# Biases folded into the projection weights, and evacuation of query/key and attention banks in one instruction each

## The reference

```
n   = layernorm(x)                           # no gain, no offset
Q,K,V = n W_Q^T + b_Q, n W_K^T + b_K, n W_V^T + b_V     # 16 heads of 64
A   = softmax(Q K^T / 8) V                   # per head, 256 x 256 scores
x1  = x + layernorm(sum over heads of A W_O + b_O)
m   = layernorm(x1)
gate = softmax(m G^T);  t = m U^T            # 8 experts, rank 16
z   = m W^T + (1/16) sum_e gate_e t_e V_e
out = x1 + layernorm(z)
```

## Time and profile before

| | |
|---|---|
| median of 3 runs | 1256.75 us (1256.18 to 1256.93) |
| the profiled execution | 1255.58 us, its span 1253.8 us |
| busy share of the span | TensorE 96%, VectorE 90%, ScalarE 83%, GpSimd 57% |
| mean granted TensorE clock | 0.990 |
| chain of work that ended last | TensorE 63%, VectorE 25%, issue 7%, GpSimd 3%, ScalarE 1% |

### The profile page before, as it was taken

One profiled execution on the slowest core, in us unless ns is written; L12 is line 12 of the kernel. 1 busy time (PEld: TensorE's weight loads), 2 busy tenths in 40 slices (PEclk: granted clock), 3 DMA queues, 4 the chain that ended last, 5 costly groups with the idle time before them and its releaser, 6 DMA issues.

```text
span 1253.8 us, 33748 instructions
## 1 busy us (share of the span) xinstructions
PE 1200.7 (96%) x10496; PEld 967.9 (77%) x10496; DVE 1124.9 (90%) x3305; ACT 1039.4 (83%) x3465; POOL 712.7 (57%) x805
## 2 busy tenths in 40 slices
PE   5999999999999999999999999999999999999994
PEld 4777787777787787887778787778887777887773
DVE  6799999999999999999999999999999999999993
ACT  6888888888888888889888888888889888889881
POOL 2456655666655666655666555666555566556552
PEclk9999999999999999999999999999999999999997
DMA  6000000000000000000000000000000000000000
GB/s 209 1 2 6 6 4 0 4 4 4 4 4 0 4 4 4 4 3 1 4 4 4 4 0 4 4 4 4 4 0 4 4 4 4 4 0 4 4 5 9
DMA packets 9925, 10.96 MB, mean 9 GB/s; under 512 B 816, under 2 KB 9392, under 8 KB 9904
## 3 DMA queue, kind: packets, MB, share of 16 engines
q1 hardware_dynamic: 9904, 10.70, 2.6%
HBM read 6.50 MB, written 4.19 MB: 9 GB/s over the span
## 4 chain that ended last, share of the span: by engine, by line
PE 63%; DVE 25%; issue 7%; POOL 3%; ACT 1%; DVEq 1%; DMA 0%; POOLq 0%; ACTq 0%
PE o_ps L313 15%; PE st_ps L287 14%; PE st_ps L297 13%; DVE neg_max L684 7%; DVE y L644 4%; PE qk_ps L259 3%; PE qk_ps L261 3%; PE qk_ps L260 3%; POOL probs L894 3%; DVE probs_t L696 3%; PE extra_ps L238 3%; DVE stats L631 2%; PE extra_ps L273 2%; PE extra_ps L274 2%; PE extra_ps L275 2%
## 5 line engine op out<-in xcount | busy, mean ns | idle before, releaser
L894 POOL TENSOR_TENSOR probs<-probs,inv_sum 128x512 f32<-128x512 f32 x512 | 529.7, 1040 | 490.8 <-DVE inv_sum L691 490.8
L494 ACT ACTIVATE probs<-st_ps,neg_max 128x256 f32<-128x256 f32 x1024 | 475.7, 478 | 20.0 <-DVE neg_max L684 15.5
L684 DVE TENSOR_REDUCE neg_max<-st_ps 128x2 f32<-128x512 f32 x512 | 337.5, 679 | 25.6 <-PE st_ps L287 22.9
L297 PE MATMUL st_ps<-ident,probs 128*128 128x128 f32 x2048 | 294.2, 279 | 13.6 <-POOL probs L894 13.5
L297 PEld LDWEIGHTS st_ps<-ident,probs 128*128 128x128 f32 x2048 | 223.5, 141 | 74.5 <-issue 36.5
L313 PE MATMUL o_ps<-probs_t,v_sb 128*64 128x256 f32 x2048 | 256.3, 387 | 0.1
L502 ACT COPY probs_t<-st_ps 128x512 f32<-128x512 f32 x256 | 151.4, 592 | 79.9 <-PE st_ps L297 79.7
L494 ACT ACTIVATION_READ_ACCUMULATOR probs<-st_ps,neg_max 128x1 f32 x1024 | 212.5, 208 | 0.0
L313 PEld LDWEIGHTS o_ps<-probs_t,v_sb 128*64 128x64 f32 x2048 | 132.9, 136 | 73.3 <-issue 5.5
L287 PE MATMUL st_ps<-k_hi,q_hi 64*128 64x256 f32 x1024 | 174.5, 329 | 13.2 <-DVE probs_t L696 6.3
L696 DVE COPY probs_t<-st_ps 128x512 f32<-128x512 f32 x256 | 173.8, 679 | 11.8 <-PE st_ps L297 11.7
(11 more groups left out here) (90 smaller groups left out, 2341.3 us busy)
## 6 DMA issues: line engine op xcount, KB each, us to landing
out<-x_all SPq DMA_DIRECT2D x32, 128.0 KB, 1.7
x_all<-in_x SPq DMA_DIRECT2D x1, 3840.0 KB, 17.5
stage_v<-in_w_v SPq DMA_DIRECT2D x1, 512.0 KB, 4.5
stage_o<-in_w_o SPq DMA_DIRECT2D x1, 512.0 KB, 6.9
stage_q<-in_w_q SPq DMA_DIRECT2D x1, 384.0 KB, 4.9
stage_k<-in_w_k SPq DMA_DIRECT2D x1, 384.0 KB, 5.8
x_all<-in_x SPq DMA_DIRECT2D x2, 128.0 KB, 3.3
ffn<-in_ffn_w SPq DMA_DIRECT2D x1, 196.0 KB, 7.0
```

Source lines behind the costliest of these rows:

```text
L297: last = nc.tensor.transpose(st_ps[p % 2][h][:, s * T + j * P:s * T + (j + 1) * P], probs[p % N_PROBS][h][:, j, s * P:(s + 1) * P], ident[ ...
L494: last = nc.scalar.activation(probs[n][h][:, j, :], st_ps[p % 2][h][:, j * T:(j + 1) * T], ACT.Exp, bias=neg_max[n][h][:, j:j + 1], accum_ ...
L684: nc.vector.tensor_reduce(neg_max[p % N_PROBS][h][:, :], st_ps[p % 2][h][:, :].rearrange("p (j s) -> p j s", j=NT), AX.X, ALU.max, negate= ...
L894: nc.gpsimd.tensor_tensor(probs[n][h][:, :, :], probs[n][h][:, :, :], inv_sum[n][h][:, :].unsqueeze(2).to_broadcast([P, NT, T]), ALU.mult) ...
```

## The change

A row of `xn` has mean zero, so adding 1 to every element of it and taking its mean out of every weight column leaves the product as it was, and adding `b/128` to all 128 rows of a weight column then adds exactly `b` to the product. The kernel makes such weights on chip, at the start. GpSimd builds diagonal matrices of the biases (`diagonals`, in SBUF of the later `probs` tiles). TensorE multiplies them by a matrix of 1/128 and adds the weights times a matrix of -1/128, both in plain fp32 (`weight_means`, eight pieces in `MEANS`, of 256, 256, 512, 512, 256, 512, 256 and 512 columns, two matmuls each). VectorE adds each piece to the weights (`fold_means`), and only then `weight_hi` and `weight_lo` split them. `xt_high` and `xt_low` add the 1. In the loop `qk_hi`, `qk_lo`, `attention_hi` and `attention_lo` become one instruction of 512 columns each. The orders of all four bodies are written anew.

```diff
-        q_hi, q_lo, k_hi, k_lo = [P, T] each, N_QK buffers
+        qk_hi_sb = [sb(f"qk_hi{n}", [P, 2 * T], F32R) for n in range(N_QK)]
+        qk_lo_sb = [sb(f"qk_lo{n}", [P, 2 * T], F32R) for n in range(N_QK)]
+            def weight_means(n, cols, bank, dst):
+                nc.tensor.matmul(bank[:, dst], mean_w[:, :], diag(n, cols),
+                                 start=True, stop=False)
+                nc.tensor.matmul(bank[:, dst], neg_mean_w[:, :], stage[n][:, cols],
+                                 start=False, stop=True).then_inc(mean_projected, 1)
             def transpose_xn(b, free):
...
                 transpose_tiles(extra_ps, xn).then_inc(x_transposed, 1)
+                if first(b):
+                    for n in "qk":
+                        pe.wait_ge(diag_ready[n], 1)
+                        pe.wait_ge(early_loaded[n], 16)
+                    for piece in MEANS[0:2]:
+                        weight_means(*piece)
             def project_qk(b, p, free):
...
+                if first(b) and p == 0:
+                    pe.wait_ge(diag_ready["v"], 2)
+                    pe.wait_ge(w_loaded["v"], 16)
+                    for piece in MEANS[2:4]:
+                        weight_means(*piece)
+                if first(b) and p == 1:
+                    pe.wait_ge(mean_folded, 4)
+                    for n, pieces in (("q", MEANS[4:6]), ("k", MEANS[6:8])):
...
+                            weight_means(*piece)
             def scores(b, p, free0, free1):
...
+                if first(b) and p == 0:
+                    pe.wait_ge(mean_folded, len(MEANS))
             def weight_hi(n, cols, loaded, ready):
-                act.wait_ge(loaded[n], 16)
+                if n == "o":
+                    act.wait_ge(loaded[n], 16)
+                else:
+                    act.wait_ge(mean_folded, loaded)
             def xt_high(b):
...
-                nc.scalar.copy(xt_hi[:, :], extra_ps[:, 0:T]).then_inc(xt_hi_ready, 1)
+                nc.scalar.activation(xt_hi[:, :], extra_ps[:, 0:T], ACT.Identity,
+                                     bias=one[:, 0:1]).then_inc(xt_hi_ready, 1)
             def qk_hi(b, p):
                 act.wait_ge(qk_projected, PAIRS * b + p + 1)
-                nc.scalar.activation(q_hi[n][:, :], qk_ps[p % 2][:, 0:T], ACT.Identity, bias=...)
-                nc.scalar.activation(k_hi[n][:, :], qk_ps[p % 2][:, T:2 * T], ACT.Identity, bias=...)
+                nc.scalar.copy(qk_hi_sb[p % N_QK][:, :], qk_ps[p % 2][:, :]).then_inc(qk_hi_ready, 1)
             def attention_hi(b, group):
-                two nc.scalar.activation of 256 columns with bias
+                nc.scalar.copy(o_hi[:, 2 * group:2 * group + 2, :].rearrange("p g q -> p (g q)"),
+                               o_ps[:, :]).then_inc(o_hi_ready, 1)
+            def fold_means(first_piece, end):
+                for count in range(first_piece, end):
+                    n, cols, bank, src = MEANS[count]
+                    dve.wait_ge(mean_projected, count + 1)
+                    nc.vector.tensor_tensor(stage[n][:, cols], stage[n][:, cols], bank[:, src],
+                                            ALU.add).then_inc(mean_folded, 1)
             def stats_x(b):
...
                     ln_apply(LN_X, xn, x_all).then_inc(xn_ready, 1)
+                    fold_means(0, 2)
             def xt_low(b):
-                nc.vector.tensor_tensor(xt_lo, extra_ps, f32(xt_hi), ALU.subtract)
+                nc.vector.scalar_tensor_tensor(xt_lo, extra_ps, 1.0, f32(xt_hi), ALU.add, ALU.subtract)
                 if first(b):
+                    fold_means(2, 4)
                     weight_lo("v", every, w_hi_ready, w_lo_ready)
             def qk_lo(b, p):
-                two nc.vector.scalar_tensor_tensor of 256 columns with bias
+                nc.vector.tensor_tensor(qk_lo_sb[n][:, :], qk_ps[p % 2][:, :], f32(qk_hi_sb[n][:, :]),
+                                        ALU.subtract).then_inc(qk_lo_ready, 1)
                 if first(b) and p == 0:
+                    fold_means(4, 8)
                     weight_lo("q", late, w_hi_ready, w_lo_ready)
             def attention_lo(b, group):
-                two nc.vector.scalar_tensor_tensor of 256 columns with bias
+                nc.vector.tensor_tensor(o_lo (512 columns), o_ps[:, :], f32(o_hi), ALU.subtract)
             def norm_x(b):                      # GpSimd
                 if first(b):
+                    for pair in (0, PAIRS // 2):
+                        diagonals("v", B_V, pair, pair + PAIRS // 2)
+                    for n, column in (("q", B_Q), ("k", B_K)):
+                        diagonals(n, column, 2, PAIRS // 2)
+                        diagonals(n, column, PAIRS // 2, PAIRS)
                     return
+            pool.wait_ge(bias_loaded, 16)       # GpSimd, ahead of its body
+            pool.wait_ge(constants_ready, 1)
+            for n, column in (("q", B_Q), ("k", B_K)):
+                diagonals(n, column, 0, 2)
```

337 lines of the change are left out of this document (172 added, 165 removed).

## The result

The changed kernel takes 1284.22 us (median of 4 runs, 1284.11 to 1284.72), the kernel before 1256.47 beside it: ratio 1.0224, 95% interval 1.0206 to 1.0241. It is slower by 2.2%; 1230 us and a gain were forecast. The profiled execution took 1284.16 us, with a span of 1282.4.

What follows compares the result with a forecast made beforehand. TensorE was taken to bound the loop, with VectorE close behind. From a span of 1253.8 us, loop -33, start +8 and tail -2 gave 1226.8; plus 1.8 and 1.2, about 1230 us, range 1220 to 1241.

Steps and rivals of the forecast that it cites:

- the period's sum: Loop: 35.7 us of TensorE blocks plus 1.0 of waiting make a period of 36.7 us, 1.07 less than before.
- What bounds the kernel: Old loop: TensorE bounds it, busy 37.20 of 37.80 us, VectorE close behind at 34.98; 1.4 us per period is waiting.
- ScalarE and VectorE in the loop: Joined loop instructions: ScalarE's load per period falls from 32.2 to 29.1 us, VectorE's from 35.0 to 32.9.
- TensorE's order, the block sum: Loop body on TensorE: 42 blocks for 44 take 35.7 us, 0.7 less than 36.4.
- TensorE's order, the waiting: New loop order: 0.75 us of named waits at T4, S6 and T5; 1.0 in all, between 0.4 and 1.9.
- The loop in all: 31 periods, each 1.07 us shorter: -33 us.
- The start: Before the loop: mean matmuls and folds put first scores at 24.3 us for 16.48; +8 us, bounds +5 and +16.
- The tail: After the loop: fewer blocks left ahead of the last chain, so fewer waits; -2 us, between 0 and -4.
- rival 1: Loop: the new order waits as much or more, 2.24 us, period 37.94; slower, 1268 us; chance 0.15.
- Rival 2: Start: the mean matmuls run at the slow clock, so it costs about 15 us; 1236 us; chance 0.13.
- Rival 4: Loop: a 512-column subtraction takes the pair's 0.78 us, so joining doesn't pay; only order gains, 1241 us; chance 0.10.

Runs made afterwards that it cites:

- e1: Changed kernel (folded weights, joined 512-column instructions) with the four loop orders of the kernel before: 1266.39 us, period 37.65.
- e8: Changed kernel with the normalisation of x1 done on one column of each tile instead of 128: 1269.96 us, period 37.86.
- e4: Changed kernel with norm_x1 moved on VectorE ahead of pair 5's invert_sum: 1294.04 us, period 38.63.
- e9: Changed kernel with the normalisations of both x1 and y done on one column of each tile: 1268.86 us, period 37.81.
- e3: Changed kernel with GpSimd's V diagonals waiting until xn is normalised and ScalarE's activation table load brought forward: 1286.46 us.
- e2: Kernel before with only the four new loop orders, no folding or joining: 1309.8 us, period 39.43.
- e14: Kernel before with pair 4's head-0 reciprocal moved between y's normalisation and its addition on VectorE: 1251.44 us, period 37.67.
- e11: e1's kernel with GpSimd's V diagonals behind xn and ScalarE's table load ahead of its waits: 1266.20 us.

## Why the prediction was wrong

The step that failed is the period's sum: "35.7 us for the body" and on top of it "What remains is the waiting of the new order", with its "I take 1.0 us of waiting, between 0.4 (near what is forced) and 1.9". The period came out at 38.3 for 36.7. The waits that the rows show are 1.7 us for 1.0, the excess being the waits for `o_lo` and x1n; the other 0.9 us is in blocks that the sum had too short.

- *What bounds the kernel*: right that TensorE bounds the old loop and VectorE is close behind. It was left at averages; the stretch in which the new order makes VectorE full was never drawn up.
- *ScalarE and VectorE in the loop*: the prices were right, 597 and 680 ns for the joined instructions, 592 and 679 forecast. In the old order ScalarE's and VectorE's period loads fall by 2.4 and 2.2 us (the earlier trace rows and e1's 29.88 and 32.82), 3.1 and 2.15 forecast. In the new order VectorE's falls by 0.5 only: the gate, x1n and `var_eps` take 1.6 us a body more in their new places beside GpSimd. The forecast kept every other instruction at its old price.
- *TensorE's order, the block sum*: 35.7 forecast, 36.6 in the trace without the four waits. The T of one head (2.82 us for six, 2.3 forecast), u ahead of S and O make the difference for the most part.
- *TensorE's order, the waiting*: the places that it named were about right. It had 0.3 at T4, 0.25 at S6 by ScalarE and 0.2 at T5; measured are 0.42, 0.21 and, ahead of S7', about 0.1 (T6' takes 0.62 there for 0.53; it is within the 36.6). What it had no place for are `o_lo` ahead of PV2, 0.51, and x1n, 0.55, together 1.06 where it allowed 0.25 for VectorE being "late at some more". x1n's wait comes with its price of 869 ns in the new place; its row, 442 ns in before, is read nowhere in the forecast. e8 prices x1n's work there at 0.46 us a period, 14.3 us of the time; what the longer duration alone costs isn't separated, since e4 changed the order with it. `o_lo`'s wait is VectorE's queue, whose relief in e9 GpSimd took back.
- *The loop in all*: 1.6 us a period too long, 47 us in 30 periods, of a miss of 54.
- *The start*: +8 forecast, +15.2 measured. The folding is some 12 to 13 of it (16 in one pair) and the order 3.5. The forecast stopped at the first scores, put at 24.3 and measured at 26.3; behind them body 1 lost another 5.4 us, of which the moved S6 and T5 are 0.91 + 0.87. Ahead of the first scores, xn's normalisation takes 2.05 us beside GpSimd's diagonals where it took 0.60, which is 1.45 of the 2.0, and the activation table load of 1.28 stands behind the fold. e3 took both away and had the first scores 1.0 earlier, so they are worth that together:

```profile
4.96 5.17 POOL L928 TENSOR_TENSOR probs<-ident,bias 128x512 f32<-128x512 f32 x6
```

```profile
5.03 2.05 DVE L698 TENSOR_SCALAR xn<-x_all,mean_var,rstd 128x128 f32<-128x128 f32 x2 [1.19 <-POOL rstd L936]
```

```profile
10.15 1.28 ACT L513 ACT_TABLE_LOAD   x1 [10.15 <-DVE stage_q L679]
```

- *The tail*: -2 forecast, -1.6 measured.
- *Rivals*: rival 1 is what happened, in kind: slower, by waiting in the stretch behind S4. PV2 did slip by a late VectorE; S6's 0.21 is ScalarE's, and T5 and S7' hardly slipped. It stopped at 2.24 us of waiting on 35.7 and 1268. Against it was said that "both engines get two to three us of air". That was the false argument: e2 shows that without this air the order costs 1.64 us a period, and with it still 0.67. Rival 2 is no cause: the forecast had a fifth of the later 40 units at the slow level, and so it came. Of the V means the first eight units are slow (1.70 us for four, 0.86 at the fast level), the rest and the late ones fast:

```profile
14.03 1.91 PE L268 MATMUL st_ps<-probs,mean_w 128*128 128x512 f32 x2
15.73 1.76 PE L270 MATMUL st_ps<-stage_v,neg_mean_w 128*128 128x512 f32 x2
17.33 1.02 PE L268 MATMUL st_ps<-probs,mean_w 128*128 128x512 f32 x2
```

- *Rival 4*: its premise is false, 680 ns for the subtraction, yet its result is true in the old order, for another reason: TensorE is the bound there, and what joining freed on the other two engines is worth 0.14 us a period.

What stays open: which part of the 0.9 us in the block sum is waiting; how the 5.4 us behind the first scores divide between the splits of the late weights and the first body's latencies; which of the joined instructions e2 lacks most. Whether PV2 would be on time with VectorE truly relieved there is open too, since e9's relief did not arrive; a version of the new order with another block between S5 and T4 was not tried.

## What to carry to other kernels

Average load doesn't tell what an order costs: before moving blocks of the bounding engine, list what the next engine does in the stretch where the blocks come together, and count the latency from the producer (here S4) to its return (T4) against the work in between. A faster instruction off the bounding engine is worth what its waits are worth, 4 us here; price a one-time cost against that first. Look up, too, which instructions of one engine come to lie beside those of another: here three unchanged VectorE instructions took 1.6 us a body more. In queues served in order, test each move alone: the pair of moves removed both waits that it aimed at and lost 18 us, and one of the two alone gained 4 to 5.

## What the hardware showed

The normalisation (two per-partition operands, 128x128, SBUF to SBUF) takes 344 ns alone (e4), 442 in before, 869 beside GpSimd's 1.04 us scalings and 1.06 us for xn beside its diagonals, a factor of two and a half to three for an instruction that had not changed. The gate's scaling of 128x8 took 228 ns in before and 609 in after. GpSimd's scaling itself took 1040 ns on average in before and in after, and 1056 in e14. The Trainium skill (SBUF — State Buffer, section Who interferes with whom) says that GpSimd shares a pair of ports with VectorE's instructions in a two-port mode and with those that have two inputs in SBUF, and that whoever comes first holds it for the whole instruction. The traces agree as far as the VectorE instruction that comes second goes: of x1n's two, one began at 629.77 and ended at 630.85, 0.09 after GpSimd's scaling, and in e9 the addition, with two inputs in SBUF, began at 618.19 and ended at 619.19, 0.27 after GpSimd's. Which mode the normalisation runs in no run shows. So an edit that moves a VectorE instruction in time can change its price, and work taken out of VectorE can come back as longer instructions.

The activation table load takes 1.28 us. In the kernel before it begins at 0.74, ahead of the first activation's wait for the biases (that activation runs at 3.07), when ScalarE had nothing else to do. In after it begins at 10.15, behind the wait for the first folded weights. In e3 and e11, with an activation of one column ahead of that wait, it begins at 0.74 again.
